# One expert per 128 slots in place of one per 256 in a routed unit of a macaron block's mixture of experts

## The reference

```python
def _L0_ffn_ref(x, gate_w, w1, w2, w3):          # E = 8 experts, H = 256 hidden, TOPK = 2
    flat = x.reshape(-1, d)
    probs = jax.nn.softmax(flat @ gate_w.T, axis=-1)
    weights, idx = jax.lax.top_k(probs, TOPK)
    weights = weights / jnp.sum(weights, axis=-1, keepdims=True)
    combine = jnp.sum(jax.nn.one_hot(idx, E, dtype=flat.dtype) * weights[..., None], axis=1)
    h1 = jnp.einsum('nd,ehd->neh', flat, w1)
    h3 = jnp.einsum('nd,ehd->neh', flat, w3)
    y = jnp.einsum('neh,edh->ned', jax.nn.silu(h1) * h3, w2)
    out = jnp.einsum('ned,ne->nd', y, combine)

x = x + 0.5 * _L0_ffn_ref(_layernorm(x), gate_w, w1, w2, w3)
x = x + _L0_attn_ref(_layernorm(x), WQ, WK, WV, WO)
x = x + 0.5 * _L0_ffn_ref(_layernorm(x), gate_w, w1, w2, w3)
```

## Time and profile before

| | |
|---|---|
| device time, median of 3 runs | 617.2 us (616.16 to 620.45) |
| the profiled execution | 616.21 us, of which its span is 613.7 us |
| busy in the span | PE 514.6 us (84%), DVE 373.7 (61%), ACT 310.0 (51%), POOL 257.5 (42%) |
| instructions | 19025, of them 7286 matmul passes, each with a weight load |
| DMA | 72.15 MB, mean 118 GB/s |

### The profile page before, as it was taken

The page is one execution under the profiler, slowest core; times in us unless marked ns, Lnnn a source line. Parts: engine busy times, 40 slices in busy tenths (PEclk is TensorE's granted clock), DMA queues, the critical chain, the costliest instruction groups (busy, mean ns, idle before and its releaser), DMA issues.

```text
span 613.7 us, 19025 instructions
## 1 busy us (share of the span) xinstructions
PE 514.6 (84%) x7286; PEld 416.7 (68%) x7286; DVE 373.7 (61%) x995; ACT 310.0 (51%) x597; POOL 257.5 (42%) x322
## 2 busy tenths in 40 slices
PE   2779859999998588888889886769689899999995
PEld 1667848889987355555556554546368789989994
DVE  5633933343355868989899988666356333356665
ACT  5843523344334256666666764555554234345543
POOL 7565364630563133433341111454614530555562
PEclk9999998999999589999999999998999999999999
DMA  9991297646965213746213110311134656543232
GB/s 269 307 323 35 81 277 118 137 129 146 165 153 142 80 42 95 198 126 179 90 38 97 38 55 3 123 34 33 32 79 97 138 133 130 140 131 98 67 89 56
DMA packets 124981, 72.15 MB, mean 118 GB/s; under 512 B 51936, under 2 KB 118752, under 8 KB 124896
## 3 DMA queue, kind: packets, MB, share of 16 engines
q1 hardware_dynamic: 117984, 56.78, 35.4%
q0 software_dynamic: 6912, 14.17, 9.3%
HBM read 18.88 MB, written 34.87 MB: 88 GB/s over the span
## 4 chain that ended last, share of the span: by engine, by line
PE 35%; DVE 17%; issue 4%; ACT 3%; another core or an unknown queue 2%; DMA 1%; DVEq 1%; POOL 0%; ACTq 0%; POOLq 0%
PE bank L1629 8%; DVE negmax L1310 7%; PE bank L1510 5%; PE bank L1512 5%; PE bank L1511 4%; PE bank L1742 2%; PE bank L1805 2%; ACT pt L958 2%; PE bank L1820 2%; PE bank L1772 2%; PE bank L1808 1%; PE bank L1759 1%; DVE rden L1327 1%; PE bank L1522 1%
## 5 line engine op out<-in xcount | busy, mean ns | idle before, releaser
L1197 DVE SCALAR_TENSOR_TENSOR pt<-bank,pt 128x512 f32<-128x512 f32 x122 | 84.2, 691 | 152.6 <-PE bank L1512 69.4
L708 POOL DMA_INDIRECT yg<-sorted_y,row x108 | 104.2, 965 | 146.9 <-PE bank L1629 64.2
L958 ACT ACTIVATE pt<-bank 128x768 f32<-128x768 f32 x128 | 103.8, 811 | 87.7 <-PE bank L1781 81.8
L694 POOL DMA_INDIRECT sorted_x<-xs,row x108 | 106.2, 984 | 90.0 <-DVE pt L1197 32.3
L1629 PE MATMUL bank<-w,pt 128*128 (+1 forms) x976 | 131.8, 277 | 7.6 <-issue 5.4
L1629 PEld LDWEIGHTS bank<-w,pt 128*128 128x128 f32 x976 | 119.7, 192 | 13.6 <-issue 10.0
L1310 DVE TENSOR_REDUCE negmax<-bank 128x10 f32<-128x640 f32 x128 | 104.1, 817 | 30.6 <-PE bank L1759 26.7
L841 ACT ACTIVATE pt<-bank 128x512 f32<-128x512 f32 x122 | 73.2, 600 | 57.3 <-PE bank L1512 38.9
L1742 PE MATMUL bank<-zc 63*64 63x64 f16 (+3 forms) x1024 | 44.4, 251 | 28.0 <-DVE negmax L1310 22.9
L849 ACT ACTIVATE yb<-bank 128x256 f32<-128x256 f32 x82 | 31.5, 384 | 67.9 <-PE bank L1629 43.2
L1742 PEld LDWEIGHTS bank<-zc 63*64 63x64 f16 x1024 | 19.4, 108 | 55.7 <-DVE negmax L1310 37.0
(11 more groups left out here) (171 smaller groups left out, 1014.1 us busy)
## 6 DMA issues: line engine op xcount, KB each, us to landing
sorted_y<-yb SPq DMA_DIRECT2D x82, 128.0 KB
zc<-qk_rows SPq DMA_DIRECT2D x96, 64.0 KB
sorted_x<-zeros SPq DMA_DIRECT2D x2, 2944.0 KB
qk_rows<-qksplit SPq DMA_DIRECT2D x8, 512.0 KB
sorted_x<-zeros SPq DMA_DIRECT2D x1, 2432.0 KB, 11.3
sorted_x<-zeros SPq DMA_DIRECT2D x1, 2176.0 KB, 10.2
X<-x_in SPq DMA_DIRECT2D x8, 256.0 KB, 5.3
zc<-w_up SPq DMA_DIRECT2D x8, 256.0 KB, 7.1
```

The source lines that it names most:

```text
L694: ps.indirect_dma_start(out=sorted_x[s], out_offset=bass.IndirectOffsetOnAxis(ap=row[:, s, k, t:t + 1], axis=0), in_=xs[:, R0[s] + t, :], ...
L708: ps.indirect_dma_start(out=yg[:, a % D_YG, k, :], out_offset=None, in_=sorted_y[s], in_offset=bass.IndirectOffsetOnAxis(ap=row[:, s, k, t ...
L958: s_.activation(pt[:, hg, (u % 2) * 768:(u % 2 + 1) * 768].rearrange("p (a n) -> p a n", a=2), bank[:, B_ST:B_ST + 2, 0:384], ACT.Exp, sca ...
L1197: v_.scalar_tensor_tensor(hid[:, n % D_HID], bank[:, B_H3 + n % 2, :], 1.0 / WSCALE, silu[:, n % D_H], ALU.mult, ALU.mult).then_inc(prod_d ...
```

## The change

A tile of 256 slots stays the unit of transposing load, silu, product and store, but it now consists of two blocks of `BLK` = 128 slots, each with its own expert. An expert's rows are rounded up to 128, so a set has at most 31, 39, 39 or 27 blocks, which is 16, 20, 20 and 14 tiles: 70 routed units in place of 82, 110 units in place of 122 (16 + 36 before attention, 34 + 24 after it). `woffset` holds an offset per block. On the way up each product over 256 columns becomes two over 128 with weights of their own; on the way down the four products are the same in size, and each half takes its own offset. The number of column loads follows the blocks. Tables that count units (paces, `first_step`, the normalising units) are adapted.

```diff
@@ -65,10 +65,13 @@
 D0 = (12, 26)
 DT = (4, 6)
 BLOCKS = tuple(n // 2 for n in DT)
-NT = tuple((2 * n * P + E * (SLOTS - 1)) // SLOTS for n in RT)
+BLK = 128
+PER = SLOTS // BLK
+NB = tuple((2 * n * P + E * (BLK - 1)) // BLK for n in RT)
+NT = tuple(-(-n // PER) for n in NB)
 NTMAX = max(NT)
 RTMAX = max(RT)
-ETILES = RTMAX * P // SLOTS
+EBLKS = RTMAX * P // BLK
 
 Y_TILE = tuple(sum(NT[:s]) for s in range(SETS))
 Y_SECOND = Y_TILE[SECOND]
...
@@ -387,7 +390,7 @@
                    [(s, t, k) for s in (2, 3) for t in range(RT[s]) for k in range(2)])
 
         def gather_unit(p, d):
-            return U_TILE[3] + 2 + 9 * d // 13 if p else U_TILE[1] + 2 + 7 * d // 10
+            return U_TILE[3] + 2 + 8 * d // 13 if p else U_TILE[1] + 2 + 7 * d // 10
 
         assert gather_unit(0, 2 * EARLY - 1) + 2 * LAG < U_SECOND
         assert gather_unit(0, len(GATHERS[0]) - 1) < U_SECOND
...
@@ -413,7 +416,7 @@
 
         def first_step(n):
 
-            return {27: (0, 0), 30: (0, 1), 33: (0, 2), 36: (0, 3), 52: (1, 0), 54: (1, 1), 56: (1, 2)}.get(n, (None, None))
+            return {27: (0, 0), 30: (0, 1), 33: (0, 2), 36: (0, 3), 47: (1, 0), 49: (1, 1), 51: (1, 2)}.get(n, (None, None))
 
         def score_bank(b, q, u):
 
...
@@ -678,7 +681,7 @@
             def first_pace(n):
 
                 if n >= FREE:
-                    pool.wait_ge(prod_done, done((n - FREE) * 7 // 10, D_H))
+                    pool.wait_ge(prod_done, done((n - FREE) * 6 // 10, D_H))
                 elif n >= 4 and n % 2 == 0:
                     pool.wait_ge(rg_ready, min(GROUPS, 3 + n // 2))
 
...
@@ -1141,7 +1144,7 @@
                 n = RT[s]
                 dve.wait_ge(m0_ready, done(M0_SUMS[s]))
                 total = bank[:, B_M0, n * E:(n + 1) * E]
-                link(v_.tensor_tensor(over[:, :, :], total.unsqueeze(2).broadcast_to([P, E, ETILES]),
+                link(v_.tensor_tensor(over[:, :, :], total.unsqueeze(2).broadcast_to([P, E, EBLKS]),
                                       bounds[:, :, :], ALU.is_gt))
                 link(v_.tensor_reduce(ntiles[:, :], over[:, :, :], AX.X, ALU.add))
                 link(v_.tensor_tensor(shares[:, :, :], ntiles[:, :].unsqueeze(1).broadcast_to([P, E, E]),
...
@@ -1163,7 +1166,7 @@
 
             def tile_experts(s):
 
-                n = NT[s]
+                n = PER * NT[s]
                 link(v_.tensor_tensor(passed[:, 0:n, :], tile_no[:, 0:n, :],
                                       start[:, 1:E].unsqueeze(1).broadcast_to([P, n, E - 1]),
                                       ALU.is_ge))
...
@@ -1430,11 +1433,11 @@
                     k_low(g, g)
                 if n == 22:
                     dve.wait_ge(y_added, done(Y_DENSE[1] - 1, D_Y))
-                if n in (22, 48):
-                    attention_norm(n // 48)
-                if n in (24, 50):
+                if n in (22, 45):
+                    attention_norm(n // 45)
+                if n in (24, 46):
                     for t in range(TILES):
-                        normalise(n // 50, t, TILES * ORDER[n // 50] + t)
+                        normalise(n // 46, t, TILES * ORDER[n // 46] + t)
                 paced_adds(0, unit)
 
 
...
@@ -1580,11 +1583,11 @@
 
             def weight_columns(s, count=None):
 
-                i0 = len(columns[s])
-                i1 = min(NT[s], i0 + (count or NT[s]))
+                i0, end = len(columns[s]), PER * NT[s]
+                i1 = min(end, i0 + (count or end))
                 if i0 == i1:
                     return
-                base = Y_TILE[s] - (Y_SECOND if s >= SECOND else 0)
+                base = PER * (Y_TILE[s] - (Y_SECOND if s >= SECOND else 0))
                 regs = [column_regs[(base + i) % COLUMNS] for i in range(i0, i1)]
                 pe.wait_ge(tiles_done, s + 1)
                 pe.load(regs, woffset[0:1, s, i0:i1])
...
@@ -1615,20 +1618,23 @@
                                                 (h3_ready, prod_done, B_H3, w3h, w3l)):
                     pe.wait_ge(read, freed(n))
                     for c in range(2):
-                        cols = bass.ds(columns[s][i] + c * P, P)
-                        last = split_product(bank[:, b0 + n % 2, c * SLOTS:(c + 1) * SLOTS],
-                                             wh[:, cols], wl[:, cols], x[:, 0], x[:, 1])
+                        for v in range(PER):
+                            cols = bass.ds(columns[s][PER * i + v] + c * P, P)
+                            toks = slice(v * BLK, (v + 1) * BLK)
+                            c0 = c * SLOTS + v * BLK
+                            last = split_product(bank[:, b0 + n % 2, c0:c0 + BLK],
+                                                 wh[:, cols], wl[:, cols], x[:, 0, toks], x[:, 1, toks])
                     last.then_inc(ready, 1)
                     if between is not None and ready is h1_ready:
                         between()
 
-            def down(n, offset):
+            def down(n, offsets):
                 pe.wait_ge(prod_done, done(n, D_H))
                 for u in range(2):
                     for c in range(2):
                         last = t_.matmul(y_half(n)[:, u * D:(u + 1) * D],
                                          hid[:, n % D_HID, c * SLOTS + u * P:c * SLOTS + (u + 1) * P],
-                                         w2[:, bass.ds(offset + c * D, D)], start=u + c == 0, stop=c == 1,
+                                         w2[:, bass.ds(offsets[u] + c * D, D)], start=u + c == 0, stop=c == 1,
                                          skip_group_check=True)
                 last.then_inc(y_ready, 1)
 
...
@@ -1638,7 +1644,7 @@
                 if s == 0 and i < 2:
                     pe.wait_ge(y_weighted, 2 * (Y_DENSE[1] - 1 + i))
                 pe.wait_ge(y_copied, freed(Y_TILE[s] + i))
-                down(U_TILE[s] + i, columns[s][i])
+                down(U_TILE[s] + i, columns[s][PER * i:PER * (i + 1)])
 
             def dense_down(p, n):
                 e = dense_unit(p, n)[1]
...
@@ -1876,11 +1882,11 @@
                             for use in (max_use(b) + 1, max_use(b) + 2):
                                 pe.wait_ge(m1_freed, use)
                                 no_use(pe, use, m1_ready)
-                    if b == ROUTED + 2:
+                    if b == ROUTED + 2 or b == ROUTED + 3 and u < 2:
                         weight_columns(2, PIECE)
 
             def second_columns(slot):
-                if slot >= NT[0] - 8:
+                if slot >= LAG + 5:
                     weight_columns(1, PIECE)
 
             def first_groups(n):
```

More of the change, by code:

```diff
@@ L142, in build_macaron @@
         value_row = sb("value_row", [P, 2 * D // 32, 32], F32)
-        bounds = sb("bounds", [P, E, ETILES], F32)
+        bounds = sb("bounds", [P, E, EBLKS], F32)
         before = sb("before", [P, E, E], F32)
-        tile_no = sb("tile_no", [P, NTMAX, E - 1], F32)
+        tile_no = sb("tile_no", [P, PER * NTMAX, E - 1], F32)
         stats = sb("stats", [P, TILES, 6], F32)
@@ L171, in build_macaron @@
         chosen = sb("chosen", [P, RTMAX + 1, E], BF16)
-        over = sb("over", [P, E, ETILES], F32)
+        over = sb("over", [P, E, EBLKS], F32)
         ntiles = sb("ntiles", [P, E], F32)
@@ L175, in build_macaron @@
         start = sb("start", [P, E], F32)
-        passed = sb("passed", [P, NTMAX, E - 1], F32)
-        expert = sb("expert", [P, NTMAX], F32)
-        woffset = sb("woffset", [P, SETS, NTMAX + 1], I32)
+        passed = sb("passed", [P, PER * NTMAX, E - 1], F32)
+        expert = sb("expert", [P, PER * NTMAX], F32)
+        woffset = sb("woffset", [P, SETS, PER * NTMAX], I32)
         place = sb("place", [P, RTMAX, E], F32)
@@ L620, in routing_constants @@
                 ps.memset(before[:, :, :], 1.0).then_inc(consts, 1)
-                ps.iota(bounds[:, :, :], pattern=[[0, E], [SLOTS, ETILES]], base=0, channel_multiplier=0,
+                ps.iota(bounds[:, :, :], pattern=[[0, E], [BLK, EBLKS]], base=0, channel_multiplier=0,
                         allow_small_or_imprecise_dtypes=True).then_inc(consts, 1)
-                ps.iota(tile_no[:, :, :], pattern=[[1, NTMAX], [0, E - 1]], base=0, channel_multiplier=0,
+                ps.iota(tile_no[:, :, :], pattern=[[1, PER * NTMAX], [0, E - 1]], base=0, channel_multiplier=0,
                         allow_small_or_imprecise_dtypes=True).then_inc(consts, 1)
@@ L764, in _ @@
             for d in range(2 * RT[3]):
-                pool.wait_ge(prod_done, done(U_TILE[2] + LAG + 6 * d // 10, D_H))
+                pool.wait_ge(prod_done, done(U_TILE[2] + LAG + 5 * d // 10, D_H))
                 scatter(3, d // 2, ks=[d % 2])
@@ L1151, in places @@
                 v_.scalar_tensor_tensor(place[:, 0:n, :],
-                                        start[:, :].unsqueeze(1).broadcast_to([P, n, E]), float(SLOTS),
+                                        start[:, :].unsqueeze(1).broadcast_to([P, n, E]), float(BLK),
```

(2 more changed lines are left out.)

## The result

| | median us | lowest to highest | profiled execution | span |
|---|---|---|---|---|
| before | 617.4 | 616.2 to 620.5 (4 runs) | 616.2 | 613.7 |
| after | 643.1 | 640.6 to 647.0 (4 runs) | 647.0 | 645.0 |

The ratio is 1.039, 95% interval 1.034 to 1.044: the change makes the kernel slower by 26 us, where 614.5 (605 to 631) was forecast. The time lies outside the range, on the side of the slower rivals. The profiled execution is the longest of the four, so the spans lie 31.3 us apart and the medians 25.7.

The account below looks back on a forecast made before the run. TensorE's array bounds the routed stretches, and its sequencer would after the change. Terms -26.4 + 20.2 + 6.1 - 4.3 + 1.3 + 0.7 = -2.4 us led to 614.5 us, range 605 to 631.

Parts of the forecast that it names:

- the slower rivals: Two alternatives: narrow products not streaming at 56 ns (630 us, chance 0.15), and more instructions, more stalls (621 us, 0.08).
- Fewer units, -26.4: Routed stretches: 12 fewer units at 2.20 us each save 26.4 us.
- Narrower products: Routed way up: 24 products of 128 columns at 0.056 us take 1.34 in place of 1.31; array's unit 2.23 us.
- The rival at 630: Routed way up: narrow products do not stream at 56 ns; midway, 77 ns, the unit is 2.74 us; chance 0.15.
- The sequencer as the bound: Routed units: TensorE's sequencer, at 2.51 us per unit, replaces the array, at 2.23, as the bound.
- the term for more register operations, +20.2: Routed stretches: more register operations at 0.113 us raise 65 intervals from 2.20 to 2.51 us, +20.2 us.
- Column loads, +6.1: Routed stretches: 17 weight-column loads at 0.65 us exposed, less 5 us already paid, net +6.1 us (bounds +3 and +13).
- Projections in the shade: Routed stretches: projections and sums run in the sequencer's shadow, -4.3 us (bounds -6 and 0).
- The moved projection, +1.3: Second group's projection: transposes come two units after the statistics' product instead of four; TensorE waits for xn, +1.3 us.
- Attention, +0.7: Attention: set 2's 10 loads in place of 6, a quarter of their cost coming through, +0.7 us (0 to 3).
- More instructions, more stalls: Rival: "issue" stalls on the down products grow with the instruction count; doubled they add 7 us, 621 us; chance 0.08.
- What would show it: Timeline signs: routed down products 2.5 us apart, dense units 2.20, register operations 0.11 through a whole unit, clock 1.00.

Follow-up runs that it names:

- after_again: The changed kernel unaltered, run once more on a chip without stalls: 587.5 us, ratio 1.010, beside 580.7 for the kernel before.
- c_fused: Changed kernel with register addresses packed ahead of the products, columns fetched eight at a time: 626.0 us (1.009); again on the chip without stalls 559.2 (0.962).
- a_one: Changed kernel with both halves of a routed unit taking the first half's weights, ten register operations per unit in place of twenty: 625.8 us, 1.007.
- a_loads: Changed kernel with weight columns fetched eight at a time, 18 loads in place of 35: 643.8 us, ratio 1.033.
- b_direct: Kernel before with POOL's 216 indirect DMAs replaced by direct ones of the same bytes, chip without stalls: 579.7 us, 0.999; again 579.5, 0.998.
- b_narrow: Kernel before with each 256-column product on the way up issued as two of 128 at the same address: 633.0 us, 1.018; again 633.0, 1.021.
- c_direct: Changed kernel with packed addresses and direct DMAs for POOL's indirect ones: 560.0 and 560.1 us without stalls; third run, chip with stalls, 560.8, ratio 0.906.

## Why the prediction was wrong

**Which chip.** The forecast was made from a trace of a chip with stalls and holds for it. The account of the 25.7 us: 6.9 are what the change costs without stalls (after_again); the other 18.8, a difference between chips, are what it adds in stalls.

**Fewer units, -26.4**: right. c_fused_again has that and the wider array unit: -26.4 + 70 x 0.084 = -20.5; measured -21.4.

**Narrower products**: right at 0.056 us, for 24 in a row. The rival at 630 isn't seen. The Trainium skill's "TensorE: Matmul & The Clock Gate", section on the back-to-back issue gap, gives 81 ns for such a stream; no trace here shows them. The array's unit is 2.287 and not 2.23 for another reason: in single records of c_fused_again, the second pass of the way down starts 0.165 us behind the first, where other passes are 0.112 apart; in the kernel before, behind wide products, all eight are. Behind narrow products the way down thus costs 0.055 us more per unit, not foreseen.

**The sequencer as the bound**: right, and shown by a_one and c_fused. **The first step that failed is the size of the term for more register operations, +20.2.** I took the floor of the spacing, 0.113, for the mean. In after_again 0.112 to 0.115 stands between most steps of a unit, 0.120 between the packed ones, but two or three in each unit take 0.15 to 0.30. Over the 34 routed units there that hold all their 22 steps and no column load, a unit takes 2.68 us on average (2.58 to 2.79), 0.122 a step. The term is then 65 x (2.68 - 2.20) = +31.2 in place of +20.2, and with it the forecast of -2.4 becomes +9, near the 6.9 of after_again. The row that I read was the best case: the eight steps of the earlier trace rows, 0.81 us from first to last, are the fastest of all 82 such groups in the trace of before. (The median there is 1.10, but most of these are held back by the array, so that trace could not give the mean of a saturated sequencer.)

**Column loads, +6.1**: right in size for the changed kernel. In after_again a unit with a column load takes 3.27 us in the median of 17, 0.6 more than one without. The first stretch is 34 x 2.68 + 2 x 0.89 + 10 x 0.65 = 99.4, measured 99.6; the second 31 x 2.68 + 2 x 2.20 + 7 x 0.65 = 92.0, measured 91.8. Wrong in kind: the price is mostly by the register, not by the load (a_loads). **Projections in the shade**: right; the two sums leave no room for them.

**The moved projection, +1.3**: as forecast in the run that was measured, where the wait for xn at L1509 is 1.5 us and did not exist before. Without stalls it is not there: in after_again the same transposes, at 176.3 us, wait 0.03 us (0.55 in c_fused_again, whose units are shorter). With +31.2 for the register operations and without this term, the sum is +7.3 where after_again has 6.9; that it comes so close is partly luck, as the loads and the shade are estimates.

**Attention, +0.7**: 247.0 against 245.2 us in b_direct on the chip without stalls, within the bounds; +5.8 where it was measured.

**More instructions, more stalls**, 0.08 and 7 us: more stalls were the case, and the greater failure is here. The sum had nothing for them, and the measured run has 18.8 us more. It was sized by the stalls on down products in the earlier trace rows, 8.3 us, in the routed stretches alone. Stalls also sat in attention and ahead of the first routed tile; the whole kernel before is 37 us longer than on the chip without them (617 against 581). And its mechanism was incomplete: the number of instructions alone does not start them, POOL's indirect DMAs are needed. b_narrow shows that TensorE's stream has a part in how much they cost: the same 216 indirect DMAs, and 6 us more. The last dense stretch is 8 us longer with unchanged code; in the changed kernel 13 gathers have to go out per 8 units in place of per 9, one each 1.35 us at 2.20 us per unit, close to the 1.25 us in which POOL can issue one (0.96 + 0.30), so rows of four and more stand there. The prediction had this number, 2.1 us of gathers per unit of 2.2, and read it only as POOL keeping up. That the denser rows are why those stalls came is argued from the order of events and from c_direct_third, where they are gone with the indirect DMAs; a slower pace alone was not tried, and which part of the change adds stalls stays open.

**What would show it**: register operations at 0.11 "through a whole unit" didn't hold, dense units at 2.20 held where nothing stalled, clock 1.00 only outside the bursts.

**Best version.** c_fused is 3.8% under the kernel before on the chip without stalls (559.2 against 580.7) and 0.9% over it where stalls are. c_direct doesn't route and counts only as a measurement: at 560.8 us on a chip with stalls it is some 65 us under c_fused on the first one (626.0), an estimate of what stalls cost that kernel.

## What to carry to other kernels

When work is cut into smaller pieces with addresses from registers, count the sequencer's steps per piece at their mean in a busy stretch, not at their floor, and pack the address arithmetic ahead of the products; here, without stalls, that is worth 28 us of 588. Compare stretches whose code did not change first: a difference there points away from the edit's own price. A kernel tuned beside stalls from another engine's DMAs holds a large hidden term, which an edit elsewhere can raise: here from some 37 us to 56.

## What the runs showed of the hardware

- With POOL's indirect DMAs in the program, neighbouring weight loads of TensorE stand 0.6 to 1.4 us apart in places in bursts of up to ten, on two of the three chips timed apart; on the other one the same kernels run 6 to 11% faster (617 against 581, 626 against 559). In c_fused 22 of 35 such pairs begin in rows of four indirect DMAs or more, under 1.36 us apart, in the kernel after 12 of 32. With direct DMAs of the same packets and bytes they are gone but for one in attention (c_direct_third).
- In the burst of the kernel after that is shown above, the granted clock went to its lower level (0.67 on average in 128 to 132 us) and stayed there behind it (0.50 in 132 to 134).
- Narrow fp16 products stream at 0.056 us for 24 in a row; the first fp32 pass behind them costs 0.055 more.
- A register load of four columns takes 0.33 us, of eight 0.59 or more. An instruction that packs several register operations is 74 ns long at most (c_fused_again, the same view as for the loads):

```profile
L1624 PEldq FUSED_REGOPS  x160: 42/74/74, 97.7 to 172.6; - x160
```
